# Second half unrolled, with x1, attention output and x2 split to 16-bit rows and transposed by DMA

## The chip, the core and the metric

The kernel runs on one core of a Trainium2 chip. The metric is the device time of one execution in microseconds (us). The core has five engines: TensorE (PE in the profile, its weight loads PEld), VectorE (DVE), ScalarE (ACT), GpSimd (POOL) and SyncE (SP), which here issues nearly all DMAs on one queue that 16 DMA engines serve. Engines wait for each other and for DMAs by semaphores, and each executes its instructions in order.

## The reference

One decoder layer, with the normalisation after each sublayer, over x (8 x 512 rows of 512) and a context (8 x 512 rows of 1024):

```
x1 = layernorm(x  + self_attention(x))          # over the axis of 8, 16 heads, relative positions
k, v = split(ctx @ W_src.T + b_src)             # 8 heads of 64, masked keys
q    = (x1 @ W_tgt.T + b_tgt) * mask
o    = softmax(q k.T / 8) v
x2 = layernorm(x1 + concat(x1, o) @ W_out.T + b_out)
out = layernorm(x2 + relu(x2 @ w1.T + b1) quantised @ w2.T + b2)
```

## The kernel before

Everything that TensorE multiplies in 16 bits is held as a pair of 16-bit tiles, a high part and a low part (value minus high part), and a product of two pairs is three matmuls (`terms`, line 44). A matmul contracts over partitions, so each activation that enters one must stand transposed, features on partitions.

The first half (`phase_a`, planned step by step by `FirstHalf`, line 301) computes x1 and the keys and values. It transposes its own activations by DMA: ScalarE writes the high part of a tile of 128 rows (`row_hi`, line 647), GpSimd the low part (`row_lo`, line 541), into one of a ring of three pairs `rows16`, and SP issues two DMA transposes (`turn`, line 455). DVE does the self-attention. x1 is stored as 32-bit rows in DRAM, keys (`kT_scratch`) and values (`v_scratch`) as 16-bit pairs.

The second half (`phase_b`, line 829) runs over the 8 batches b, each with 512 rows in four tiles tt of 128. Batch b of the attention is interleaved with the feed-forward of batch b-1 (`heads(b, ff)`, line 1146 on PE, 1287 on ACT, 1432 on DVE). At the boundary between two batches PE does, in this order:

- `feed_forward2` (four outputs of 16 matmuls with eight-bit operands), with the last head's `values` between the second and third;
- 16 transposes of the attention output o (`transposes`, line 1031, with the 32-bit identity, `b_st<-ident,k` and the like), one PSUM bank per tile; ACT and DVE make the pair `oT` from PSUM;
- `output_x1` (line 1134): 48 matmuls x1T by the first half of W_out, no end of the sum yet;
- the branch of the hardware loop (`Fori`), then 16 transposes of the next x1 (`x1_transposes`, line 1046), which SP loaded as 32-bit rows into `x1n` long before;
- `output_rest` (line 1184): 52 matmuls that add o's share and the bias; DVE adds the residual into `x2` (`residual`, line 1472), GpSimd makes the factors of the norm (`layer_norm_factors`, line 79), ACT applies them (`normalize`, line 1245);
- `queries` of the next batch (12 matmuls each), with 16 transposes of x2 ahead of the fourth, then the first scores, then `feed_forward1(ff, 0)`, the first reader of `x2T`.

SP's queue in the loop (lines 995 to 1003): the copies of the queries into `q1` and `q2` (18 DMAs in three groups, `queries`, line 953), the load of x1, mask and keys (`load_heads`, line 922, after the last `p_lo` of the batch) and values (five DMAs, after `av_filled`), the stores of four output tiles, and four loads of the residual rows (`load_residual`, line 947), each of which waits until the store from the same rows has landed. In the names of the profile `q` stands for what lives in `w.q` (x1n, x2) and also for q1/q2, `k` for what lives in `w.k` (o, pf) and k1/k2.

Of the kernel before, what the change touches and what calls it, by code (L numbers as in the profile page):

```python
# [64 lines left out]
def all_stored(sp, w):  # L65

    for i in range(2):
        sp.wait_ge(w.st_out[i], 16 * 2 * 8 * NBATCH // 2)
    for i in range(3):
        sp.wait_ge(w.x1_out[i], 16 * len(range(i, NB * T, 3)))  # L70

# [229 lines left out]
class FirstHalf:  # L301

    STEPS = 16 * NB + 4
# [33 lines left out]
    def uses(self, g):  # L337

        b, t = g // 16, g % 8
        out = [("o", n) for n in self.tiles(g - 1)]  # L340
        if b < NB - 1 and (1 <= g % 16 <= 8):
            out.append(("x", 8 * (b + 1) + g % 16 - 1))
        return out + [("c", n + 5) for n in self.quarters(g) if n + 5 < QUARTERS]
# [6 lines left out]
    def loads_after(self, g):  # L350

        return [use for use in self.uses(g + 1) if use[0] != "o"]
# [15 lines left out]
def phase_a(nc, ctx, d, w):  # L368
# [34 lines left out]
    turned = [sem(f"A_turned{i}") for i in range(RING)]  # L403
# [10 lines left out]
    x1_o = w.x1_d.rearrange("t (nb p) e -> nb t p e", p=P)  # L414

# [9 lines left out]
    def row_source(kind, i):  # L425

        return {"x": xn[i % 2], "c": cn[i % 2], "o": ctx1}[kind][:, :]
# [13 lines left out]
    with nc.Block() as block:  # L441
        @block.sync
        def _(sp):
# [11 lines left out]
            def turn(kind, i):  # L455
# [32 lines left out]
            def load_residual(n):  # L488
                if n >= 3:
                    sp.wait_ge(x1_out[n % 3], 16 * (n // 3))  # L490
                sp.dma_start(x1[n % 3][:, :], x_in[n // T, n % T]).then_inc(res_ld[n % 3], 16)
# [15 lines left out]
            for g in range(plan.STEPS):  # L507
# [17 lines left out]
                if g == 16 * (NB - 1) + 13 and w.b_ld is not None:  # L525
                    for n in range(0, NB * T, T):
                        sp.wait_ge(x1_out[n % 3], 16 * (n // 3 + 1))
                    sp.dma_start(w.x1n, w.x1_d.rearrange("b (tt p) e -> b p tt e", p=P)[0]).then_inc(w.x_ld, 16)
# [117 lines left out]
        def _(act):  # L646
            def row_hi(kind, i):
# [5 lines left out]
                elif kind == "c":  # L653
                    act.wait_ge(cn_ld[i % 2], 16 * (i // 2 + 1))
                else:
# [173 lines left out]
def phase_b(nc, ctx, d, w):  # L829
# [20 lines left out]
    x1n, x2 = w.x1n, w.q[:, 4:8, :]  # L850
    o, pf = w.k[:, 0:4, :], w.k[:, 4:8, :]
    x1T = pair("x1T", [P, KT, B])
# [36 lines left out]
    names = ("xt_filled", "xt_hi", "xt_lo", "q_filled", "q_masked", "q_hi", "q_lo", "m_made", "sx_filled", "sx_max",  # L889
             "negm", "mr_filled", "mr_copied", "st_filled", "st_exp", "p_hi", "p_lo", "av_filled", "o_rden",  # L890
             "o_norm", "ot_filled", "ot_hi", "ot_lo", "om_filled", "om_used", "x2t_filled", "x2t_hi", "x2t_lo",
# [7 lines left out]
    xr_ld = [sem(f"B_xr_ld{i}") for i in range(4)]  # L899
    out_st = [sem(f"B_out_st{i}") for i in range(4)]  # L900
    w1_ld, w2_ld = ([sem(f"B_{n}_ld{i}") for i in range(4)] for n in ("w1", "w2"))
    alone = {e: sem(f"B_alone_{e}") for e in ("sp", "dve", "pe", "act")}
# [15 lines left out]
    with nc.Block() as block:  # L918
        @block.sync
        def _(sp):  # L920
            def load_heads(b, first):

                if not first:
                    sp.wait_ge(s["p_lo"], 16 * b)
                    stand_alone(sp, alone["sp"])
# [8 lines left out]
                else:  # L934
                    sp.wait_ge(s["av_filled"], 8 * b)
                    stand_alone(sp, alone["sp"])
# [5 lines left out]
            def load_x1(b):  # L942
                sp.wait_ge(s["xt_filled"], 4 * b)
                stand_alone(sp, alone["sp"])
                sp.dma_start(x1n[:, :, :], x1_in[b]).then_inc(w.x_ld, 16)

            def load_residual(b, tt, first):
                if not first:
                    sp.wait_ge(out_st[tt], 16 * b)
                    stand_alone(sp, alone["sp"])  # L950
                sp.dma_start(x2[:, tt, :], x1_in[b][:, tt, :]).then_inc(xr_ld[tt], 16)

            def queries(b, g):
# [3 lines left out]
                stand_alone(sp, alone["sp"])  # L957
# [7 lines left out]
            def store(b, tt):  # L965
                sp.wait_ge(s["l3_done"], 4 * b + tt + 1)
                stand_alone(sp, alone["sp"])
# [20 lines left out]
            load_x1(1)  # L988
# [15 lines left out]
            last = NBATCH - 1  # L1004
            for g in range(len(GROUPS)):
                queries(last, g)
            for tt in range(4):
                store(last - 1, tt)
            for tt in range(4):
# [588 lines left out]
```

## Time and profile before

| | |
|---|---|
| median of 3 runs | 2004.89 us (2004.09 to 2007.42) |
| the profiled execution | 2004.7 us |
| its span in the trace | 2002.9 us |
| PE busy | 1861.0 us, 93% of the span |
| DVE busy | 1344.8 us, 67% |
| ACT busy | 784.5 us, 39% |
| POOL busy | 490.0 us, 24% |
| mean granted TensorE clock | 0.968 of 2.4 GHz |

The first half ends near 881 us of the span; the second half takes the rest. A matmul's record of 0.38 us overlaps its neighbours; how fast matmuls follow each other is read from the starts. A row of a timeline gives start, length, engine, line, operation, output<-inputs and count, and in brackets the idle time before it with what ended it. Rows of SPq are the issuing of DMAs on SP's sequencer, not the transfer; the time from issue to landing is listed apart.

### The profile page before, as it was taken

What the parts mean: (1) busy time and instruction counts of PE and PEld (TensorE: products, weight loads), DVE (VectorE), ACT (ScalarE), POOL (GpSimd) and SP (SyncE); (2) the same over time, 40 slices, a digit from 0 to 9 for tenths busy, and PEclk for the clock granted to TensorE, in tenths of its full rate; (3) what the DMA queues carried; (4) which work ended last, traced back from release to release, by engine and by line L of the source; (5) the groups of instructions that cost most, each with busy time, mean ns of one, the idle gap of its engine ahead of it and who ended that gap; (6) DMA issues with size and microseconds to landing.
All of it is one profiled execution on the core that took longest, in us unless ns stands there. A gap on an engine that the chain in (4) does not pass through costs nothing. (4 is left out here: it accounts for less than half of the span.)

```text
span 2002.9 us, 33372 instructions
## 1 busy us (share of the span) xinstructions
PE 1861.0 (93%) x12588; PEld 1022.7 (51%) x12588; DVE 1344.8 (67%) x1698; ACT 784.5 (39%) x1209; POOL 490.0 (24%) x546
## 2 busy tenths in 40 slices
PE   5998999899989897977899999999999999999998
PEld 5554565456545564544545545455455554554543
DVE  3499987898799879866665565564655555556531
ACT  3432222122222211136646265363562644635522
POOL 1334662475357423720000100001001000010010
PEclk7998999899989998989999999999999999999999
DMA  6543366335634445556420413304105142041010
GB/s 221 118 115 80 95 141 143 74 100 136 142 82 95 117 97 170 144 127 199 92 63 2 109 45 58 96 1 101 53 6 112 38 84 70 1 101 32 7 37 21
DMA packets 290831, 176.60 MB, mean 88 GB/s; under 512 B 194793, under 2 KB 248041, under 8 KB 290690
## 3 DMA queue, kind: packets, MB, share of 16 engines
q1 hardware_dynamic: 286320, 174.17, 34.6%
q8 instruction: 114, 1.87, 0.4%
q10 hardware_dynamic: 4370, 0.34, 0.2%
q14 instruction: 27, 0.22, 0.0%
HBM read 94.75 MB, written 33.55 MB: 64 GB/s over the span
## 5 line engine op out<-in xcount | busy, mean ns | idle before, releaser
L1351 DVE TENSOR_TENSOR p_lo<-k,p_hi 128x1024 f16<-128x1024 f32 x128 | 156.8, 1225 | 193.6 <-ACT p_hi L1239 193.6
L81 POOL TENSOR_TENSOR vsb<-mvb,consts 128x1 f32<-128x1 f32 x64 | 12.1, 190 | 1031.0 <-DVE mvb L1366 1031.0
L1040 PE MATMUL b_ff<-x2T_hi,w1T_hi 128*128 128x512 f16 x512 | 195.0, 381 | 2.3 <-DVE x2T_lo L1351 2.3
L1396 DVE CUSTOM_DVE_ANT_0 junk<-b_sx,mneg 128x512 f16<-128x512 f32 x256 | 175.8, 687 | 31.0 <-issue 22.4
L1040 PE MATMUL b_ff<-x2T_lo,w1T_hi 128*128 128x512 f16 x512 | 194.9, 381 | 0.0
L1040 PE MATMUL b_ff<-x2T_hi,w1T_lo 128*128 128x512 f16 x512 | 194.8, 381 | 0.0
L1271 ACT ACTIVATE k<-b_st,mbias 128x512 f32<-128x512 f32 x256 | 161.5, 684 | 15.0 <-PE b_st L1084 15.0
L619 PE MATMUL sm_b<-cT_hi,wsT_hi 128*128 128x256 f16 x512 | 143.4, 280 | 16.7 <-DMA cT_lo<-rows_lo 16.7
L741 DVE TENSOR_TENSOR prod<-q,k 128x4096 f32<-128x4096 f32 x32 | 141.9, 4433 | 22.0 <-ACT q L673 11.0
L1239 ACT ACTIVATE p_hi<-k 128x1024 f16<-128x1024 f32 x128 | 135.3, 1057 | 44.3 <-PE b_av L1099 41.9
L591 PE MATMUL pj_b<-winT_hi,xT_hi 128*128 128x512 f16 x384 | 146.6, 382 | 3.9 <-DMA xT_lo<-rows_lo 3.9
L1263 ACT ACTIVATE hq<-b_ff,b 128x512 fp8e4<-128x512 f32 x128 | 88.0, 687 | 156.0 <-PE b_ff L1040 149.1
L591 PE MATMUL pj_b<-winT_lo,xT_hi 128*128 128x512 f16 x384 | 146.6, 382 | 0.0
L591 PE MATMUL pj_b<-winT_hi,xT_lo 128*128 128x512 f16 x384 | 146.4, 381 | 0.0
L619 PE MATMUL sm_b<-cT_lo,wsT_hi 128*128 128x256 f16 x512 | 143.3, 280 | 0.0
L619 PE MATMUL sm_b<-cT_hi,wsT_lo 128*128 128x256 f16 x512 | 143.2, 280 | 0.0
L779 DVE TENSOR_TENSOR prod<-pr,v 128x4096 f32<-128x4096 f32 x32 | 142.1, 4442 | 0.5
L746 DVE TENSOR_REDUCE pr<-prod 128x128 f32<-128x4096 f32 x32 | 141.5, 4421 | 1.1
L1248 ACT ACTIVATE q<-q,rstdb 128x512 f32<-128x512 f32 x64 | 52.1, 814 | 161.7 <-POOL rstdb L87 161.7
L545 POOL TENSOR_TENSOR rows_lo<-ctx,rows_hi 128x512 f16<-128x512 f32 x32 | 86.6, 2705 | 115.4 <-ACT rows_hi L657 115.4
L1040 PE MATMUL b_ff<-w2T,hq 128*128 128x512 fp8e4 x512 | 112.9, 379 | 1.6 <-ACT hq L1263 1.0
L545 POOL TENSOR_TENSOR rows_lo<-cn,rows_hi 128x512 f16<-128x512 f32 x64 | 96.0, 1505 | 73.5 <-ACT rows_hi L657 73.2
(258 smaller groups left out, 4340.4 us busy)
## 6 DMA issues: line engine op xcount, KB each, us to landing
cn<-in_ctx_dram SPq DMA_DIRECT2D x64, 256.0 KB, 3.0
k<-kT_scratch SPq DMA_DIRECT2D x24, 512.0 KB, 7.8
xn<-in_x_dram SPq DMA_DIRECT2D x32, 256.0 KB, 2.9
x<-in_x_dram SPq DMA_DIRECT2D x32, 256.0 KB, 3.0
x_scratch<-x SPq DMA_DIRECT2D x32, 256.0 KB, 2.2
q<-x_scratch SPq DMA_DIRECT2D x8, 1024.0 KB, 5.6
q<-x_scratch SPq DMA_DIRECT2D x32, 256.0 KB, 3.9
out_dram<-q SPq DMA_DIRECT2D x32, 256.0 KB, 4.1
```

What stands on the lines that cost most here:

```text
L545: pool.tensor_tensor(lo[:, :], row_source(kind, i), hi[:, :], ALU.subtract).then_inc(s["row_lo"], 1)
L591: pe.matmul(out, a, c, start=(j == 0 and m == 0), stop=False)
L619: pe.matmul(dst, a, z, start=(j == 0 and m == 0), stop=False)
L741: dve.tensor_tensor(prod[:, :, :], q[:, t, :].unsqueeze(1).to_broadcast([P, T, E]), k[:, :, :], ALU.mult).then_inc(s["sc_prod"], 1)
L746: dve.tensor_reduce(pr[:, t].rearrange("p h s -> p s h"), prod[:, :, :].rearrange("p s (h d) -> p s h d", h=H1), AX.X, ALU.add).then_inc(s ...
L779: dve.tensor_tensor(by_head(prod), probs, by_head(v), ALU.mult).then_inc(s["av_prod"], 1)
L1040: mm = pe.matmul(out, a, c, start=(start and n == 0), stop=end)
L1239: act.activation(dst, src, ACT.Copy, scale=scale).then_inc(done, 1)
L1263: act.activation(hq[:, f, :], ff_b[f % 2][:, :], ACT.Relu, bias=b1[:, f:f + 1], scale=1.0 / WS, saturate=False).then_inc(s["relu"], 1)
L1271: act.activation(pf[:, st, :], st_b[st % 2][:, :], ACT.Exp, bias=mbias[:, st:st + 1], scale=D2 ** -0.5).then_inc(s["st_exp"], 1)
L1351: dve.tensor_tensor(dst, bank, hi, ALU.subtract).then_inc(out, 1)
L1396: dve.tensor_tensor_reduce(junk[:, :], sx_b[tt % 2][:, :], mneg[:, :], 1.0, NEG, ALU.add, ALU.max, mx[:, h % 2, tt:tt + 1]).then_inc(s["sx ...
```

## The change

- The loops of the second half over batches become plain Python loops, so every batch is written out; the `stand_alone` semaphore increments go.
- PE no longer transposes x1, o and x2. A ring of three pairs `rows16b` takes the high part (ACT, `row_hi`) and the low part (DVE, `row_lo`) of each tile of o and x2, from SBUF instead of PSUM, and SP issues two DMA transposes per tile (`turn`). A fourth tile waits until the first tile's transposes have landed.
- x1 is split to 16-bit rows already in the first half: a new kind of use "n" in its plan (ACT, GpSimd, then two DMA stores to `x1_rows_scratch`), one step longer. The second half reads x1 by eight DMA transposes per batch straight from DRAM (`turn_x1`), for batch 0 within the first half (`x1T_first`), alternating between two buffers.
- `output_x1` stands after `feed_forward2` in all batches. SP's queue is in another order.

```diff
+                if kind == "n":
+                    for z in range(2):
+                        sp.dma_start(x1r_o[z, i // T, i % T], rows16[u % RING][z][:, :]).then_inc(turned[u % RING], 16)
+                    return
...
-                    sp.dma_start(w.x1n, w.x1_d.rearrange("b (tt p) e -> b p tt e", p=P)[0]).then_inc(w.x_ld, 16)
+                    for tt in range(NB):
+                        for z in range(2):
+                            sp.dma_start_transpose(w.x1T_first[z][:, :, tt * P:(tt + 1) * P],
+                                                   w.x1r_d[z, 0, tt * P:(tt + 1) * P, :]).then_inc(w.x1_turned[0], 16)
...
+            def turn(kind, b, tt):
+                u = use_no(kind, b, tt)
+                dst = x2T if kind == "x2" else oT
+                sp.wait_ge(s["row_lo"], u + 1)
...
+                for z in range(2):
+                    sp.dma_start_transpose(col(dst[z], tt), rows16[u % RING][z][:, :]).then_inc(turned[u % RING], 16)
...
-            with sp.Fori(0, NBATCH - 2) as b:
-                for g in range(len(GROUPS)):
-                    queries(b + 1, g)
-                load_x1(b + 2)
-                load_heads(b + 2, False)
+            for b in range(NBATCH):
                 for tt in range(4):
-                    store(b, tt)
-                for tt in range(4):
-                    load_residual(b + 1, tt, False)
...
+                    turn("o", b, tt)
+                if b:
+                    for tt in range(4):
+                        store(b - 1, tt)
+                    for tt in range(4):
+                        load_residual(b, tt, False)
+                turn("x2", b, 0)
+                turn("x2", b, 1)
+                if b + 1 < NBATCH:
+                    queries(b + 1, 0)
+                turn("x2", b, 2)
+                turn("x2", b, 3)
+                if b + 1 < NBATCH:
+                    queries(b + 1, 1)
+                    queries(b + 1, 2)
+                if b + 2 < NBATCH:
+                    turn_x1(b + 2)
+                    load_heads(b + 2, False)
...
-                pe.wait_ge(s["o_norm"], 8 * b + 8)
-                for tt in range(4):
-                    transposes(tq_b[tt], o[:, tt, :], s["ot_filled"])
-                if ff is not None:
-                    output_x1(ff)
+                output_x1(b, ff)
...
+            def row_hi(kind, b, tt):
+                u = use_no(kind, b, tt)
+                if u >= RING:
+                    act.wait_ge(turned[u % RING], 32 * (u // RING))
...
                 normalized(b, H2 - 1)
+                for tt in range(3):
+                    row_lo("o", b, tt)
                 feed_forward_sum(ff, 2)
+                row_lo("o", b, 3)
                 feed_forward_sum(ff, 3)
...
-                for tt in range(4):
+                residual(b, 0)
+                for tt in range(1, 4):
                     residual(b, tt)
+                    row_lo("x2", b, tt - 1)
```

PE before, at the last boundary: L1033 are the transposes of o, then the matmuls of `output_x1` (wxT is W_out, x1T the transposed x1).

```order
L1099 MATMUL b_av<-v_hi,p_lo 128x65
L1040 MATMUL b_ff<-w2T,hq 128x512 x32
L1033 MATMUL b_st<-ident,k 128x128 x8
L1033 MATMUL b_mr<-ident,k 128x128 x4
L1033 MATMUL b_av<-ident,k 128x128 x4
L1040 MATMUL b_sx<-wxT_hi,x1T_hi 128x512
```

PE now, at the same place (L1075 and L1129 are lines of the changed kernel):

```order
L1129 MATMUL b_av<-v_hi,p_lo 128x65
L1075 MATMUL b_ff<-w2T,hq 128x512 x32
L1075 MATMUL b_sx<-wxT_hi,x1T_hi 128x512
L1075 MATMUL b_sx<-wxT_lo,x1T_hi 128x512
L1075 MATMUL b_sx<-wxT_hi,x1T_lo 128x512
```

The transposes are gone, and `output_x1` follows feed_forward2 directly.

SP before, in the loop from the last value load to the end of the body (ISA and REGISTER_ALU are address and count registers of the loop), and the queries that come next:

```order
L940 DMA v_lo<-v_scratch 128x4x512
L966 ISA
L968 ISA
L968 DMA out_dram<-q 128x512
...
L951 DMA q<-x_scratch 128x512
L995 REGISTER_ALU
L995 COMPARE_AND_BRANCH
L962 DMA q<-qn_hi 64x512 x2
```

SP now, for one of the batches in the middle:

```order
L960 DMA v_lo<-v_scratch 128x4x512
L971 DMA_TRANSPOSE oT_hi<-rows16b_hi 128x4x128
L971 DMA_TRANSPOSE oT_lo<-rows16b_lo 128x4x128
...
L999 DMA out_dram<-q 128x512 x4
L984 DMA q<-x_scratch 128x512 x4
L971 DMA_TRANSPOSE x2T_hi<-rows16b_hi 128x4x128
L971 DMA_TRANSPOSE x2T_lo<-rows16b_lo 128x4x128
...
L994 DMA q<-qn_hi 64x512 x2
L995 DMA q<-qn_lo 64x512
```

Between the value loads and the stores stand eight transposes of o; before the first group of queries stand four of x2, behind it four more.

DVE now, from the residual of the third tile to the first row part behind the queries (L1487 is the residual, L1363 the subtraction that makes a low part, L1393 the masking of a query tile):

```order
L1487 SCALAR_TENSOR_TENSOR q<-b_ff,q 128x512
L1375 BN_STATS statsb<-q 128x6
L1377 BN_AGGR mvb<-statsb 128x2
L1363 TENSOR_TENSOR rows16b_lo<-q,rows16b_hi 128x512
L1487 SCALAR_TENSOR_TENSOR q<-b_ff,q 128x512
...
L1363 TENSOR_TENSOR rows16b_lo<-q,rows16b_hi 128x512
L1393 SCALAR_TENSOR_TENSOR qf<-b_st,bt,mrow 128x512
L1363 TENSOR_TENSOR qn_lo<-qf,qn_hi 128x512
L1363 TENSOR_TENSOR rows16b_lo<-q,rows16b_hi 128x512
```

Before, the four residuals followed each other with nothing between them, and the low parts of x2 were taken from PSUM in one piece after the third query tile.

## Rows read from the trace of the kernel before

**Rows 1.** Stretches: us, busy time by engine, clock, DMA share, GB/s.
```profile
1147.00:1278.00 131.00, 127.65 (x960) 66.20 (x958) 74.47 (x154) 65.89 (x95) 8.94 (x32) 1.00 0.26 59
```

**Rows 2.** Timeline of PE at the boundary after batch 1: start us, length.
```profile
1108.68 7.07 PE L1040 MATMUL b_ff<-w2T,hq 128*128 128x512 fp8e4 x32
1115.59 1.04 PE L1033 MATMUL b_st<-ident,k 128*128 128x128 f32 x8
1117.33 0.38 PE L1040 MATMUL b_sx<-wxT_hi,x1T_hi 128*128 128x512 f16 x1
...
1128.45 1.09 PE L1033 MATMUL b_st<-ident,q 128*128 128x128 f32 x8 [0.59 <-issue]
...
1130.25 0.38 PE L1040 MATMUL b_sx<-wxT_hi,oT_hi 128*128 128x512 f16 x1
...
1149.24 1.04 PE L1033 MATMUL b_sx<-ident,q 128*128 128x128 f32 x8
...
1152.91 0.59 PE L1066 MATMUL b_sx<-k,q 128*128 128x512 f16 x2
...
1155.62 0.38 PE L1040 MATMUL b_ff<-x2T_hi,w1T_hi 128*128 128x512 f16 x1
```

**Rows 3.** Timeline of SP's issuing at the same boundary.
```profile
1108.99 6.78 SPq L938 DMA_DIRECT2D v_hi<-v_scratch  x4
1115.86 0.75 SPq L940 DMA_DIRECT2D v_lo<-v_scratch  x1
...
1122.97 2.17 SPq L951 DMA_DIRECT2D q<-x_scratch  x4
1146.58 1.18 SPq L962 DMA_DIRECT2D q<-qn_hi  x2
1147.80 0.59 SPq L963 DMA_DIRECT2D q<-qn_lo  x1
```

**Rows 4.** DMA transposes of the first half (L466): duration ns min/median/max, first and last.
```profile
L466 SPq DMA_TRANSPOSE cT_hi<-rows_hi x64: 1189/1212/1541, 73.5 to 829.4; - x64
L466 SPq DMA_TRANSPOSE cT_lo<-rows_lo x64: 1251/1264/2471, 74.8 to 830.6; - x64
...
DMA to landing us min/median/max: 2.4/2.5/5.3
```

**Rows 5.** Page, DMA issues: count, KB each, median us from issue to landing.
```profile
x_scratch<-x SPq DMA_DIRECT2D x32, 256.0 KB, 2.2
...
q<-x_scratch SPq DMA_DIRECT2D x32, 256.0 KB, 3.9
...
v_lo<-v_scratch SPq DMA_DIRECT2D x8, 512.0 KB, 5.8
...
q<-qn_hi SPq DMA_DIRECT2D x64, 64.0 KB, 2.0
```

**Rows 6.** Timeline of DVE and ACT: one residual, its norm, one split of queries.
```profile
1133.36 0.69 DVE L1476 SCALAR_TENSOR_TENSOR q<-b_sx,q 128x512 f32<-128x512 f32 x1 [1.10 <-PE b_sx L1042]
...
1134.92 0.18 DVE L1366 BATCH_NORM_AGGREGATE mvb<-statsb 128x2 f32<-128x6 f32 x1
...
1136.57 0.81 ACT L1248 ACTIVATE q<-q,rstdb 128x512 f32<-128x512 f32 x1 [5.37 <-POOL rstdb L87]
...
1145.13 0.63 ACT L1239 ACTIVATE qn_hi<-qf 128x512 f16<-128x512 f32 x1 [2.23 <-DVE qf L1383]
...
1145.79 0.69 DVE L1351 TENSOR_TENSOR qn_lo<-qf,qn_hi 128x512 f16<-128x512 f32 x1 [0.69 <-ACT qn_hi L1239]
```

**Rows 7.** Stretches of 2 us around a pause of PE; columns as in rows 1.
```profile
316.00:318.00 2.00, 0.00 (x0) 0.00 (x0) 2.00 (x1) 0.22 (x1) 0.46 (x2) 1.00 1.09 214
318.00:320.00 2.00, 0.71 (x7) 0.64 (x8) 0.91 (x1) 0.82 (x2) 2.00 (x3) 0.98 0.31 55
320.00:322.00 2.00, 2.00 (x11) 1.40 (x10) 0.75 (x1) 0.38 (x1) 1.07 (x1) 0.50 0.98 130
322.00:324.00 2.00, 2.00 (x14) 1.50 (x13) 0.00 (x0) 0.00 (x0) 0.00 (x0) 0.67 0.42 59
```

**Rows 8.** Waits of PE in the whole span: us in total, times, longest.
```profile
PE b_st L1040 <- DVE x1T_lo L1351: 3.9, 1, 3.9
```

**Rows 9.** SP in batch 0: its issue of w1's fifth block.
```profile
925.25 0.63 SPq L974 DMA_DIRECT2D x2T_hi<-in_w_dram  x1
```

**Rows 10.** GpSimd's split of o in the first half: duration ns min/median/max.
```profile
L545 POOL TENSOR_TENSOR rows_lo<-ctx,rows_hi x32: 1149/1156/5210, 183.3 to 866.7; 128x512 f16<-128x512 f32 x32
```

More of the change, by code:

```diff
@@ L342, in uses @@
             out.append(("x", 8 * (b + 1) + g % 16 - 1))
+        out += [("n", n) for n in self.tiles(g - 4)]
         return out + [("c", n + 5) for n in self.quarters(g) if n + 5 < QUARTERS]
@@ L402, in phase_a @@
     s = {n: sem("A_" + n) for n in names}
-    turned = [sem(f"A_turned{i}") for i in range(RING)]
+    turned = w.turned
     res_ld = [sem(f"A_res_ld{i}") for i in range(3)]
@@ L848, in phase_b @@
     ident16 = sb("ident16", [P, P], F16)
-    x1n, x2 = w.x1n, w.q[:, 4:8, :]
+    x2 = w.q[:, 4:8, :]
     o, pf = w.k[:, 0:4, :], w.k[:, 4:8, :]
-    x1T = pair("x1T", [P, KT, B])
+    x1T = [w.x1T_first, pair("x1T", [P, KT, B])]
+    rows16 = [pair(f"rows16b_{i}", [P, E]) for i in range(RING)]
     qf = [sb(f"qf{i}", [P, B], F32) for i in range(2)]
@@ L1021, in _ @@
             pool.memset(rows_b[:, :], 0.0).then_inc(s["made"], 1)
-            with pool.Fori(0, NBATCH) as b:
+            for b in range(NBATCH):
                 for l in ("l2", "l3"):
@@ L1221, in _ @@
             heads(0, None)
-            with pe.Fori(0, NBATCH - 1) as b:
-                x1_transposes(b + 1, False)
+            for b in range(NBATCH - 1):
                 output_rest(b)
@@ L1302, in heads @@
                     normalize("l3", ff, 1)
[L1303 to L1304 removed]
+                row_hi("o", b, 3)
                 if ff is not None:
@@ L1307, in heads @@
                     normalize("l3", ff, 3)
-            def x2_hi(b):
-                for tt in range(4):
-                    hi(col(x2T[0], tt), bank4(om_b[tt]), s["x2t_filled"], 4 * b + tt + 1, s["x2t_hi"])
             for z in range(2):
@@ L1466, in queries_and_first_maximum, with row_lo @@
                 queries_low(b, 3)
-            def x1_low(b):
-                for tt in range(4):
-                    low(col(x1T[1], tt), bank4(tq_b[tt]), col(x1T[0], tt), s["xt_hi"], 4 * b + tt + 1, s["xt_lo"])
+            def row_lo(kind, b, tt):
+                u = use_no(kind, b, tt)
+                src = x2 if kind == "x2" else o
+                low(rows16[u % RING][1][:, :], src[:, tt, :], rows16[u % RING][0][:, :], s["row_hi"], u + 1, s["row_lo"])
             def residual(b, tt):
@@ L1479, in residual @@
                 moments("l2", x2[:, tt, :], n, tt)
-            def x2_low(b):
-                for tt in range(4):
-                    low(col(x2T[1], tt), bank4(om_b[tt]), col(x2T[0], tt), s["x2t_hi"], 4 * b + tt + 1, s["x2t_lo"])
             dve.memset(q2[D2:P, :, :], 0.0).then_inc(s["rows_made"], 1)
@@ L1516, in _ @@
             last = NBATCH - 1
-            for tt in range(4):
+            residual(last, 0)
+            for tt in range(1, 4):
                 residual(last, tt)
-            x2_low(last)
+                row_lo("x2", last, tt - 1)
+            row_lo("x2", last, 3)
             for tt in range(4):
```

142 lines of the change are left out of this document (64 added, 78 removed).

## The prediction

> **What bounds the kernel now.** I read the busy times by stretch first. In the second half TensorE is busy 127.65 of 131 us in a batch, at full clock, while DVE has 74 and ACT 66 [rows 1]: the reader sees that an instruction taken off PE shortens the batch, until something else is late. Next comes PE's timeline at one boundary between batches, the only place that the change touches on PE [rows 2]. Read the starts, not the lengths. The two feed_forward2 outputs start at 1108.68 and end where the transposes of o start, at 1115.59: 32 matmuls in 6.91 us, 0.216 each. Then come 16 transposes until 1117.33 (1.74 us), output_x1 with 48 matmuls (10.4 us, to 1127.7), the loop's branch and the 16 transposes of x1 (2.55 us), output_rest from 1130.25, and the first matmul on x2T at 1155.62. The third view is SP's issuing at that boundary [rows 3], where I look for what stands ahead of the new transposes. The fourth is the one place where DMA transposes already run, the first half [rows 4], for the price of their issue and landing.
>
> **What is removed.** Per batch 1.74 us (o), 2.55 us (x1, with the branch and its 0.59 us of idle) and 1.74 us (x2; 16 transposes at the rate of the eight that start at 1149.24) [rows 2]: 6.0 us. Eight batches would give 48 us if all that replaces them were hidden. The stretch from 1115.59 to 1155.62 is 40.0 us long now and would be 34.0. Sixteen transposes in 1.74 us are 0.109 us each. The Trainium skill (TensorE: Matmul & The Clock Gate, Part 4: PE-mode transpose) gives about 275 ns for a transpose of 128 x 128 in a kernel, and by that figure 48 of them would be an estimated 13 us a batch and the ceiling over 100 us. By that rule a record has the right length here (eight of them make 1.04 us), but successive ones overlap, and the trace decides for 6.0 us.
>
> **What is added at a boundary.** I follow the chain for batch 1 in the clock of the trace. Everything new passes through SP in order.
>
> 1. SP issues the value loads until 1115.86 + 0.75 = 1116.6 [rows 3]. They wait for the last `values`, as do the rows of o, so nothing of o can be turned earlier. A pair of transposes takes SP 1.21 + 1.26 = 2.5 us [rows 4]. o0 is issued by 1119.1; v_lo, ahead of it in the same queue, lands 5.8 us after its issue [rows 5], at 1121.7. I let o0 land at 1122.2; by itself it would be 1120.4 (2.5 us after the second issue at 1117.9).
> 2. The ring has three slots, so the split of o3 waits for o0: ACT 0.63, DVE 0.69 [rows 6], 1123.6. Queued behind that on DVE is feed_forward_sum(3), for whose first operation (0.69) the last tile of output_x1 waits, since it writes the same bank. It could start at 1115.59 + 36 x 0.216 = 1123.4 and starts at 1124.4. PE loses 1.0 to 1.5 us, and output_rest starts at T = 1127.3 (11.7 us after 1115.59).
> 3. SP: o1, o2, o3 until 1126.6, then four stores. A load of the residual waits for the store of the same tile to land: 2.2 us at the best row for 256 KB, then 3.9 us for the load [rows 5]: 1126.6 + 2.2 + 3.9 = 1132.7, T + 5.2 or so. Before, these loads were issued at 1122.97 [rows 3], before output_rest had begun. Now residual(0), which PE allows at T + 2.8, is 2.4 us late.
> 4. A tile of x2 costs DVE 1.8 us (residual to moments, 1133.36 to 1135.1), 3.2 us from the residual's start to the norm on ACT, then 0.81, 0.63, 0.69 [rows 6]. DVE does residual(1), but before residual(2) it stands at the low part of tile 0: ready at 5.2 + 3.2 + 0.8 + 0.6 = 9.9, done at 10.6. Residual 2 from 10.6 to 12.4, low part of tile 1 to 13.1, residual 3 from 13.1, its norm 16.3 to 17.1. Low part 2 and the first masked queries end at 16.7; the high and low part of queries 0 end at 17.7 and 18.4; x2's fourth tile is split at 18.4 (ACT) and 19.1.
> 5. SP turned x2's tiles 0 and 1 meanwhile, then waits for those queries: six DMAs, 1.18 + 0.59 and so on, 3.7 us [rows 3], 18.4 to 22.1. Tile 2 to 24.6, tile 3 to 27.1, landed at 25.8 + 2.5 = T + 28.3.
> 6. PE meanwhile: output_rest 11.2, three queries 7.8, eight matmuls 1.7, so T + 20.7; the copies of the first queries land at 19.6 + 2.0 = 21.6 [rows 5], 0.9 us of wait. The scores and four matmuls take 2.7 us (1152.91 to 1155.62), and from T + 24.3 PE waits 4.0 us for x2T.
>
> So feed_forward1 starts 11.7 + 28.3 = 40.0 us after 1115.59: as before. The six microseconds go into waits. The sum hardly depends on where o0 lands: with T earlier by 1.3, the SP chain is late by as much against it. I bound the stretch by 38.3 (loads and stores at their fastest, 1.4 and 0.3 less) and 42.
>
> **The clock.** A pause of 3.6 us in the first half, from 315.7 to 319.3, is followed by the clock at 0.50 and 0.67 [rows 7], 1.2 instead of 2.4 GHz, for some 2.7 us, which is 1.35 us lost. A pause of 4.0 us does this too, I assume: 1.4 us a boundary, with 0 and 2.8 as bounds.
>
> **The other parts.**
> - Six boundaries (after batches 1 to 6): 6 x (0.0 + 1.4) = +8.4 us; bounds -10 and +24.
> - The boundary after batch 0 has output_x1 on the other side of the values now: o's transposes, 14 us behind `values`, are covered by 10.4 us of output_x1 only. There is no store there, so x2T comes at T + 26.9 instead of 25.4. I take +1.5 with the clock (-3 to +4).
> - After the last batch no value load and no query is in SP's way: 1.74 us saved on o, but x2T is complete 9.5 us after output_rest, where PE's transposes and the splits took 7.3: +0.4 (-1.7 to +3).
> - Batch 0: the 16 transposes of x1 and the wait for x1T_lo, 3.9 us [rows 8], go: about -5 with the clock. But SP issues eight transposes (10 us; one load of 0.4 us before) ahead of w1's fifth block, which went out at 925.25 [rows 9] and which PE was already waiting for. PE gets it some 9.6 - 5 us later than now, less what slack is left: +3 in all (-5 to +6).
> - The first half: at its end x1's last tile needs ACT 0.63, POOL 1.16 [rows 10] and two stores of 0.45, +2.7 us. Eight transposes hold SP for 10 us near the end, most of it in front of a row of o that had 7 us of slack, +1. Thirty-two more splits on POOL, 64 more issues on SP and a ring of three shared by one more user: +3 (0 to +11).
> - Semaphore increments gone on DVE and PE: -2 (0 to -3).
>
> Sum: 8.4 + 1.5 + 0.4 + 3 + 6.7 - 2 = +18 us on the profiled execution's 2004.7 (span 2002.9 and 1.8 around it; the median shown is 2004.89, the same): 2022.7, say 2022. The low ends together give 1985, the high ends 2055.
>
> **The rivals.**
> A. *The stretch shortens (the other side).* If stores and reloads land at their fastest, the clock holds over pauses of under 4 us and batch 0 keeps its 5 us, the low ends hold together: about 1987. For it: SP is idle from 1125.1 to 1146.6 now [rows 3], so nobody has tried how fast this path can be. Against: it needs several links at their minimum. The point from which it decides is residual(0) at T + 3.
> B. *The transposes cost SP no more than plain copies.* With 0.45 us an issue (four reloads took 2.17 us with their waits [rows 3]), o ends by 1125, residual(0) comes 1.6 us earlier and tiles 2 and 3 of x2 need 1.8 us instead of 5: x2T lands at T + 24.4, about when PE asks. Six boundaries give 3.9 us each, batch 0 keeps its 5, and the time is about 1975. 256 transposes at 1.19 us or more speak against it [rows 4]. The Trainium skill (Advanced Engine Details and Errata, X-Bar Transpose (TRN2)) says that transpose DMAs are as fast as regular ones; in landing the trace agrees (2.5 against 2.0 to 2.2 us), in issue it does not.
> C. *Everything is hidden*, PE is the bound: 2004.7 - 48 - 4 + 3 = about 1955. It needs x2T 5 us earlier than my chain gives.
> D. *Worse than forecast*: transposes from DRAM, which the trace of before does not show, or the ring in the first half hold SP and PE longer; 2045 or more.
>
> **How the numbers follow.** Forecast, 2008 to 2040: 0.56. A: 0.18. B: 0.06. C: 0.04. D: 0.09. That the parts cancel within 0.2% (4 us, about what a measurement of this kernel can tell from no change): 0.07. Faster is A, B and C, 0.28; same 0.07; slower 0.65. The range 1986 to 2042 leaves out B, C and most of D. The forecast's own range is 2008 to 2040.
>
> **What the profile would show.** Right: PE idles about 4 us ahead of each first matmul on x2T with the transpose DMA as releaser, and about 1 us inside output_x1 behind f16o; SP issues nearly without a gap from the value loads to the residual loads, and the query copies stand between two pairs of x2T; the clock dips once a batch; a batch takes about 132 us. Wrong: a batch of 127 us or less; transposes in the second half at 0.5 us an issue; or a first half longer by over 15 us.

## The result, and the profile after

| | before | changed |
|---|---|---|
| median | 2004.49 us (2003.41 to 2007.42, 4 runs) | 2045.26 us (2042.59 to 2045.66, 4 runs) |
| span of the profiled execution | 2002.9 us | 2043.3 us |
| PE busy | 1861.0 us | 1833.9 us |
| POOL busy | 490.0 us | 536.0 us |
| mean granted clock | 0.968 | 0.955 |

The ratio is 1.0198, 95% interval 1.0181 to 1.0216: 41 us slower, where +18 was forecast and 2042 was the upper end of the range. The direction was right, and the forecast size was less than half of what came.

The stretches of the changed kernel, columns as in [rows 1]. The first is one whole batch, the second the boundary just before it (from the end of feed_forward2 to feed_forward1), the third its feed_forward1 and heads:

```profile
1180.26:1315.29 135.03, 125.81 (x917) 62.35 (x917) 72.36 (x151) 65.25 (x92) 9.65 (x32) 0.98 0.33 73
1138.46:1180.26 41.80, 33.48 (x154) 14.66 (x152) 20.35 (x41) 10.33 (x15) 7.22 (x23) 0.99 0.55 131
1180.26:1258.13 77.87, 77.04 (x652) 39.97 (x653) 41.70 (x92) 49.68 (x70) 0.00 (x0) 0.96 0.14 30
```

PE has 125.8 busy in 135.0 us, where it had 127.65 in 131 [rows 1]. The third row, 77.87 us with PE busy nearly all of it and a clock of 0.96, was 76.1 us long before. PE's timeline at the boundary after batch 1, which answers to [rows 2]:

```profile
1138.46 0.38 PE L1075 MATMUL b_sx<-wxT_hi,x1T_hi 128*128 128x512 f16 x1
...
1147.95 0.39 PE L1075 MATMUL b_ff<-wxT_hi,x1T_hi 128*128 128x512 f16 x1 [1.56 <-DVE f16o L1435]
...
1153.14 0.38 PE L1077 MATMUL b_sx<-rows_b,ones 128*128 128x512 f16 x1
...
1173.38 0.59 PE L1096 MATMUL b_sx<-k,q 128*128 128x512 f16 x2 [1.95 <-DMA q<-qn_lo]
...
1180.26 0.59 PE L1075 MATMUL b_ff<-x2T_hi,w1T_hi 128*128 128x512 f16 x1 [4.47 <-DMA x2T_lo<-rows16b_lo]
```

SP's issuing there, which answers to [rows 3]:

```profile
1131.75 8.31 SPq L958 DMA_DIRECT2D v_hi<-v_scratch  x4
1140.10 0.79 SPq L960 DMA_DIRECT2D v_lo<-v_scratch  x1
1141.00 1.23 SPq L971 DMA_TRANSPOSE oT_hi<-rows16b_hi  x1
...
1150.18 1.27 SPq L971 DMA_TRANSPOSE oT_lo<-rows16b_lo  x1
1151.49 2.04 SPq L999 DMA_DIRECT2D out_dram<-q  x4
1153.77 2.69 SPq L984 DMA_DIRECT2D q<-x_scratch  x4
1162.34 1.63 SPq L971 DMA_TRANSPOSE x2T_hi<-rows16b_hi  x1
...
1170.03 1.16 SPq L994 DMA_DIRECT2D q<-qn_hi  x2
...
1173.85 1.22 SPq L971 DMA_TRANSPOSE x2T_hi<-rows16b_hi  x1
...
1177.72 1.27 SPq L971 DMA_TRANSPOSE x2T_lo<-rows16b_lo  x1
```

Read the two together. SP issues without a gap from 1131.75 to 1156.46, the picture that the forecast drew: values, then o, then stores, then reloads. PE stands idle for 1.6 us inside output_x1, for 1.95 us before the first scores and for 4.5 us before its first matmul on x2T. The waits of PE in the whole span (us in total, times, longest):

```profile
PE om_b L614 <- DMA c1T_lo<-rows_lo: 47.5, 8, 10.4
PE b_ff L1075 <- DMA x2T_lo<-rows16b_lo: 40.1, 8, 9.2
...
PE b_ff L1075 <- DVE f16o L1435: 10.7, 6, 2.5
PE b_sx L1096 <- DMA q<-qn_lo: 10.3, 7, 1.9
PE b_ff L1068 <- DMA x2T_hi<-in_w_dram: 9.2, 1, 9.2
```

The second row is the wait for x2T at the seven boundaries (3.8 to 4.7 us each) and behind the last batch (9.2). The rows of f16o and of the query copies belong to the boundaries too. The last row is the fifth block of w1 in batch 0. The transposes of o and x2 have the issue time and the landing time of those in the first half [rows 4]:

```profile
L971 SPq DMA_TRANSPOSE oT_hi<-rows16b_hi x32: 1207/1220/1298, 1011.7 to 1951.4; - x32
...
L971 SPq DMA_TRANSPOSE x2T_lo<-rows16b_lo x32: 1190/1267/1274, 1029.0 to 1975.7; - x32
...
DMA to landing us min/median/max: 2.3/2.4/4.6
```

Where the 40.4 us between the two spans are, by the starts on PE:

| part | forecast | measured |
|---|---|---|
| first half (881.10 to 889.59) | +6.7 | +8.5 |
| batch 0 and the boundary behind it (first matmul on x2T: 1024.15 to 1046.30, less the 8.5) | +4.5 | +13.7 |
| six middle boundaries (131.78 to 134.79 a batch) | +8.4 | +18.1 |
| last boundary and the end | +0.4 | +0.2 |
| increments gone | -2 | inside the other rows |

Batch 0 has three waits of PE that it did not have before, or not at this length: the 9.2 us for w1's fifth block (1.7 before), 3.9 us for the last `p_lo`, and 5.2 us for the first oT, behind the keys and values on SP:

```profile
997.94 0.20 PE L1126 MATMUL b_av<-v_hi,p_hi 128*128 128x65 f16 x1 [3.92 <-DVE p_lo L1363]
...
1016.73 0.61 PE L1075 MATMUL b_sx<-wxT_hi,oT_hi 128*128 128x512 f16 x1 [5.22 <-DMA oT_lo<-rows16b_lo]
```

```profile
1000.80 9.91 SPq L958 DMA_DIRECT2D v_hi<-v_scratch  x4
```

### The profile page after: what moved, and what is told of

It reads as the page before. It is cut to its first block, busy times and chain, and to the rows that moved or that the text cites. A ratio compares the mean times of both kernels' runs of the same rounds, so it can differ in the third digit from the quotient of the medians.

```text
span 2043.3 us, 30887 instructions
## 1 busy us (share of the span) xinstructions
PE 1833.9 (90%) x12204; PEld 987.1 (48%) x12204; DVE 1329.4 (65%) x1666; ACT 791.5 (39%) x1209; POOL 536.0 (26%) x578
## 4 chain that ended last, share of the span: by engine, by line
PE 31%; SPq 8%; DVE 5%; DMA 5%; ACT 4%; issue 2%; POOL 1%; ACTq 0%; DVEq 0%; POOLq 0%
PE b_ff L1075 19%; SPq L971 3%; SPq L958 3%; PE b_st L1113 2%; PE b_st L1114 2%; PE b_sx L1096 2%; PE b_av L1126 2%; PE b_av L1129 1%; PE b_av L1127 1%; DVE p_lo L1363 1%; SPq L994 1%; DMA x2T_lo<-rows16b_lo 1%; DMA q<-x_scratch 1%; DMA oT_lo<-rows16b_lo 1%; PE b_sx L1075 1%
## 5 line engine op out<-in xcount | busy, mean ns | idle before, releaser
L1363 DVE TENSOR_TENSOR p_lo<-k,p_hi 128x1024 f16<-128x1024 f32 x128 | 156.6, 1223 | 192.6 <-ACT p_hi L1253 192.6
L1075 PE MATMUL b_ff<-x2T_hi,w1T_hi 128*128 128x512 f16 x512 | 200.4, 391 | 40.1 <-DMA x2T_lo<-rows16b_lo 40.1
L1075 PE MATMUL b_ff<-x2T_hi,w1T_lo 128*128 128x512 f16 x512 | 200.2, 391 | 0.0
L1075 PE MATMUL b_ff<-x2T_lo,w1T_hi 128*128 128x512 f16 x512 | 200.1, 391 | 0.0
L756 DVE TENSOR_TENSOR prod<-q,k 128x4096 f32<-128x4096 f32 x32 | 141.9, 4433 | 20.6 <-ACT q L688 12.1
L558 POOL TENSOR_TENSOR rows_lo<-cn,rows_hi 128x512 f16<-128x512 f32 x64 | 104.3, 1633 | 65.1 <-ACT rows_hi L672 64.5
L1075 PE MATMUL b_ff<-w2T,hq 128*128 128x512 fp8e4 x512 | 113.0, 379 | 0.8 <-ACT hq L1276 0.8
L1126 PEld LDWEIGHTS b_av<-v_hi,p_hi 128*128 128x128 f16 x1024 | 93.4, 98 | 32.8 <-DVE p_lo L1363 28.2
L1126 PE MATMUL b_av<-v_hi,p_hi 128*128 128x65 f16 x1024 | 101.1, 196 | 7.6 <-DVE p_lo L1363 7.4
```

Source lines behind the costliest of these rows:

```text
L558: pool.tensor_tensor(lo[:, :], row_source(kind, i), hi[:, :], ALU.subtract).then_inc(s["row_lo"], 1)
L756: dve.tensor_tensor(prod[:, :, :], q[:, t, :].unsqueeze(1).to_broadcast([P, T, E]), k[:, :, :], ALU.mult).then_inc(s["sc_prod"], 1)
L1075: mm = pe.matmul(out, a, c, start=(start and n == 0), stop=end)
L1126: pe.matmul(dst, hi[:, st, rows], v_hi[:, st, h, :], start=(st == 0), stop=False)
L1363: dve.tensor_tensor(dst, bank, hi, ALU.subtract).then_inc(out, 1)
```

## The experiments

Theory S: what is lost is lost in SP's in-order queue and in what PE waits for behind it. The rivals were that the unrolled program is slower by itself (U), that the split, norm and low-part chain of DVE and ACT sets the boundary (L), and that the clock has no part in it (K). Two more belong to one run each: that the first half loses its time by the eight transposes from DRAM and not by the rows (P), and that w1 is late for another reason than the transposes ahead of it (W). Each ratio is to the kernel before, on the same chip, with its 95% interval. Differences in us are between medians. The medians of the kernel before lay between 2003.08 and 2004.49 beside these runs, so differences under some 3 us say nothing.

**The unrolling alone.**

```
-            with pe.Fori(0, NBATCH - 1) as b:
+            for b in range(NBATCH - 1):
...
-                    stand_alone(pe, alone["pe"])
```

> The kernel before with its second-half loops written out and the lone semaphore increments gone, nothing else. Theory S (the change loses its time in SP's in-order queue and in what PE waits for behind it): the unrolling itself gives a little, seven loop branches of 0.6 us of idle on PE and some increments on DVE, so 2004.5 - 2 to - 5, 1999 to 2003 us. Rival U (the written-out program is slower by itself, for instance because instructions arrive late): 2008 us or more, and PE waits on its own sequencer in the second half.

1990.09 us, ratio 0.9922 (0.9906 to 0.9939). U is refuted, and the gain that S gave it was too small by 9 us (1999 at the low end). The edit takes out the loops and the `stand_alone` increments together, so their shares stay unknown. One batch of it:

```profile
1152.92:1282.80 129.88, 128.15 (x965) 66.81 (x964) 75.21 (x156) 66.78 (x96) 9.00 (x32) 1.00 0.24 60
```

A batch was 131.78 us on average. At the branch, output_x1 to the transposes of x1 now takes 10.36 us (1115.46 to 1125.82) where it took 11.12 to 12.02; feed_forward1 with the heads takes 75.39 in place of 76.14. So against a kernel with the same loops written out, the rest of the change costs 55 us, not 41.

**The first half alone**, and the same without the stores.

```
+        out += [("n", n) for n in self.tiles(g - 4)]
...
+                    act.wait_ge(s["ln_done"], i + 1)
```

> The kernel before with only the first half's part: x1 is also split on ACT and GpSimd and stored as 16-bit rows, which nobody reads. Theory S with the sizes of the forecast: the ring of three and GpSimd cost 3 us and the tail 2.7, so 2009 to 2012 us. Rival P (the first half's loss comes from the eight transposes of batch 0's x1 from DRAM in SP's queue): 2006 us or less.

2008.78 us, 1.0026 (1.0016 to 1.0037): 5.2 us by the ratio, where the forecast had 5.7 for this part. P wanted 2006 or less and is refuted.

```
-                        sp.dma_start(x1r_o[z, i // T, i % T], rows16[u % RING][z][:, :]).then_inc(turned[u % RING], 16)
+                    sp.sem_inc(turned[u % RING], 32)
```

> The kernel before with x1 split to 16-bit rows in the first half (ACT, GpSimd, ring, as in the run that cost 5.0 us) but the rows not stored: SP only marks them as gone. If the 5 us are SP's 64 issues and their transfers, 2004 us (before itself: 2003.5). If they are GpSimd's 32 splits and the order of the ring, 2007 to 2009 us.

2006.77 us, 1.0017 (1.0005 to 1.0030), between the two cases expected. The two intervals overlap, so the times do not tell the parts apart. The profiles, one execution each, have PE's first transpose of the second half at these starts (before; split only; split and stored; changed kernel):

```profile
881.10 1.94 PE L1033 MATMUL b_sx<-ident,q 128*128 128x128 f32 x8 [4.75 <-PEq L441]
```

```profile
881.88 1.94 PE L1043 MATMUL b_sx<-ident,q 128*128 128x128 f32 x8 [6.28 <-PEq L445]
```

```profile
885.63 1.94 PE L1044 MATMUL b_sx<-ident,q 128*128 128x128 f32 x8 [7.19 <-PEq L445]
```

```profile
889.59 1.94 PE L1068 MATMUL b_sx<-ident,q 128*128 128x128 f32 x8 [7.20 <-PEq L445]
```

That is 0.8 us for the splits, 3.7 for the stores and 4.0 for what is left in the changed kernel, batch 0's eight transposes from DRAM in place of one load. It speaks for SP rather than GpSimd, but it is one execution of each, and no run has the eight transposes alone.

**Batch 1's x1 behind the weights.**

```
-            turn_x1(1)
             sp.wait_ge(s["wq_filled"], 4)
...
             for n in range(4, FT):
                 load_weights(n)
+            turn_x1(1)
```

> The changed kernel with the eight transposes of batch 1's x1 behind the last weight load of w1 and w2 instead of ahead of the fifth. Theory S: PE's wait of 9.2 us at the fifth block of w1 goes, down to the 1.7 us of before, and the half speed behind it: 2045.3 - 7.5 - 1 = 2037 us. Rival W (weights are late for another reason, the link or the slots they are loaded into): the wait stays over 5 us and the time within 3 us of 2045.

2034.41 us, 1.0141 (1.0124 to 1.0158), 10.9 less than the changed kernel, where 8.5 were expected. The wait for w1's block is gone, and W is refuted. The wait for oT in batch 0 stays (5.9 us). The fifth block's issue in the changed kernel, behind eight transposes and four reloads, and here:

```profile
937.90 1.26 SPq L978 DMA_TRANSPOSE x1T_lo<-x_rows_scratch  x1
939.21 2.00 SPq L984 DMA_DIRECT2D q<-x_scratch  x4
941.59 0.34 SPq L1005 DMA_DIRECT2D x2T_hi<-in_w_dram  x1
```

```profile
927.27 1.85 SPq L984 DMA_DIRECT2D q<-x_scratch  x4
929.17 0.43 SPq L1005 DMA_DIRECT2D x2T_hi<-in_w_dram  x1
```

**The value loads behind the residual loads**, and the key loads alone moved there.

```
+                if b + 1 < NBATCH:
+                    load_values(b + 1)
                 turn("x2", b, 0)
                 turn("x2", b, 1)
```

> The changed kernel with the five value loads of the next batch issued after the residual loads, no longer ahead of the transposes of o. Theory S: o is turned 9 us earlier, the wait inside output_x1 (1.2 to 2.5 us) goes, the residual loads are there when output_rest has its first tile, and x2T comes 2.5 us earlier after that: 1.5 + 2.5 us a boundary and 1 us of clock, seven boundaries, 2045.3 - 35 = 2010 us, from 2005 to 2022. Rival L (the latency of residual, norm, split and transposes of x2 on DVE and ACT sets the end, not SP's queue ahead of them): only the wait in output_x1 goes, PE still waits 4.5 us for x2T, 2045.3 - 10 = 2035 us.

2005.95 us, 1.0012 (1.0002 to 1.0022): 39.3 less. S had 35, and L is refuted for the part ahead of x2. The gain is not where S had it, though: the clock gives almost nothing back (the heads still take 77.07 us), and 9.3 us of it lie in batch 0, where PE no longer waits for oT (first matmul on x2T at 1036.99 after 1046.30). The keys alone:

```
+                if b + 1 < NBATCH:
+                    load_keys(b + 1)
                 turn("x2", b, 0)
                 turn("x2", b, 1)
```

> The changed kernel with only the three key loads (512 KB each) moved behind the residual loads; the value loads stay ahead of o's transposes. In the changed kernel SP issues the four value loads in 8.3 us behind the keys, in the kernel with later values in 3.7 us. If this is the queue standing full of the keys, the values now take 3.7 us to issue, o is turned 4.6 us earlier, the wait inside output_x1 goes, and about half of the 39 us of the later values are gained: 2045.3 - 18 = 2027 us, 2018 to 2034. If the values' issue takes its 8 us by itself when they stand there, 2040 us or more.

2006.88 us, 1.0013 (1.0002 to 1.0023): 38.4 less, twice what I expected, and as much as by moving the values. SP with the keys moved:

```profile
1123.44 4.09 SPq L962 DMA_DIRECT2D v_hi<-v_scratch  x4
1127.58 0.78 SPq L964 DMA_DIRECT2D v_lo<-v_scratch  x1
1128.46 1.24 SPq L975 DMA_TRANSPOSE oT_hi<-rows16b_hi  x1
```

The four value loads take 4.09 us in place of 8.31 (2.8 to 4.2 us at all seven boundaries, 7.7 to 9.9 in the changed kernel). So half of the values' issue time came from the 1.5 MB of keys in front of them. In the changed kernel the third value load holds SP until 1138.0, and the last key load lands at 1138.6. That would fit a queue that takes no more while it is full, but no run shows its depth. The first row of o goes out at 1128.46, 1.7 us ahead of the end of feed_forward2 (1130.15). In the changed kernel it went out 2.5 us behind it. The boundary is 37.6 us (1130.15 to 1167.73) after 41.8. The chain takes the 4.2 us whole. Moving the values too gives it nearly nothing more (37.3): residual(0) then starts 3.0 us after output_rest, as early as PE allows, and with the keys moved it is 3.8. In both kernels PE still waits for x2T, 3.8 to 4.0 us with later values and 3.8 to 5.0 with later keys, and the heads still take 77 us.

**Is it the issue of a transpose?** Two kernels: plain copies of the same bytes in place of the transposes of o and x2, and one transpose for high and low part together. The first leaves out the turning itself, so its output is not the layer's.

```
-                    sp.dma_start_transpose(col(dst[z], tt), rows16[u % RING][z][:, :]).then_inc(turned[u % RING], 16)
+                    sp.dma_start(col(dst[z], tt), bank4(rows16[u % RING][z])).then_inc(turned[u % RING], 16)
```

> The changed kernel with the DMA transposes of o and x2 replaced by plain copies of the same bytes between the same buffers, so that nothing is turned there (x1's transposes from DRAM stay). Theory S (the issue time of a transpose on SP, 1.25 us against some 0.5, is what the boundary pays): the wait inside output_x1 goes (1.6), x2T comes 3 to 4 us earlier and the half clock behind the pause goes (1.7), seven boundaries of 6 to 7 us: 2045.3 - 45 = 2000 us, 1990 to 2008. Rival L (latency of the split and norm chain on DVE and ACT): PE still waits over 3 us for x2T, 2035 us or more.

2024.02 us, 1.0089 (1.0068 to 1.0111): 21 less. An issue takes 0.62 us. The time lies between what S (1990 to 2008) and L (2035 or more) had, and neither is borne out. The values are still in front, the fourth tile still waits for a place in the ring of three (f16o, 2.1 us on average), and pauses of 1.9 to 3.4 us remain before x2T.

```
+                sp.dma_start_transpose(col(both, tt), rows_both[u % RING][:, :]).then_inc(turned[u % RING], 16)
```

> The changed kernel with one DMA transpose of 128x1024 for the high and the low part together in place of two of 128x512 for o and x2. If SP's 1.25 us are a price for each issue, half of them go and the time is near that of the kernel with plain copies, 2000 to 2010 us. If they are a price for the elements, an issue takes 2.5 us, the high part can no longer go before the low one is ready, and the time stays within 6 us of 2045.

2014.59 us, 1.0058 (1.0041 to 1.0074): 31 less. Twice the elements cost SP one issue:

```profile
L972 SPq DMA_TRANSPOSE oT<-rows16b x32: 1232/1262/3331, 1008.9 to 1917.0; - x32
L972 SPq DMA_TRANSPOSE x2T<-rows16b x32: 1232/1250/1692, 1024.8 to 1943.9; - x32
```

PE waits 1.6 to 2.7 us for x2T here. Behind four of the seven pauses (1.6 to 2.3 us) the heads take 75.35 us, behind the other three (2.3 to 2.7) about 77.0. That is 6.8 of the 12.6 us by which its profiled execution beats that of the plain copies, where all seven are 76.6 or more.

**The clock alone.** 18 extra matmuls where PE waits for x2T.

```
+                        for j in range(18):
+                            pe.matmul(ff_b[0][:, :], col(wxT[0], 0)[:, j % KT], wxT[0][:, j % KT, :],
+                                      start=j == 0, stop=j == 17)
```

> The changed kernel with 18 extra matmuls (3.9 us at 0.216 each, their result is overwritten) on PE at the seven places where it waits 3.8 to 4.7 us for x2T. Theory S with the clock: feed_forward1 and the heads after it take 77.0 to 77.9 us in the changed kernel and 75.4 in the unrolled one of before; if the half clock after the pause makes this difference, the extra work gives back 1.6 to 2.5 us a boundary although nothing else is faster: 2045.3 - 13 = 2032 us, 2028 to 2037. Rival K (the longer stretch has another cause, DMA traffic or the order of ACT and DVE): 2045 us or more.

2031.78 us, 1.0142 (1.0114 to 1.0170): 13.5 less, by doing more work, whose result is overwritten. K is refuted. Stretches of 2 us on PE (busy, count, clock, DMA share, GB/s) around the wait, the changed kernel and this one:

```profile
1176.00:1178.00 2.00, 0.00 (x0) 1.00 0.59 107
1178.00:1180.00 2.00, 0.00 (x0) 0.78 0.42 94
1180.00:1182.00 2.00, 1.74 (x5) 0.50 0.36 92
1182.00:1184.00 2.00, 2.00 (x6) 0.50 0.42 106
```

```profile
1174.00:1176.00 2.00, 2.00 (x11) 1.00 0.75 125
1176.00:1178.00 2.00, 1.47 (x7) 1.00 0.34 76
1178.00:1180.00 2.00, 1.95 (x10) 1.00 0.39 98
```

In the changed kernel the clock falls from 1.00 (2.4 GHz) within the wait and is at 0.50 (1.2 GHz) from 1180 to 1184. With the extra work it stays at 1.00, and feed_forward1 with the heads takes 75.35 to 75.37 us at all seven boundaries, after 76.87 to 77.87. Over the seven that is 14 us, the whole gain.

**The first query group on ACT's queue.**

```
-                if b + 1 < NBATCH:
-                    queries(b + 1, 0)
...
+                act.wait_ge(s["q_lo"], 4 * (b + 1) + 1)
+                for a in range(2):
...
+                        act.dma_start(dst, qn[0][rows, 0:1, :]).then_inc(qs_ld[0][a], 16)
```

On the changed kernel:

> The changed kernel with only the first query group's six copies on ACT's queue; the value loads stay ahead of o's transposes. Theory S: in the changed kernel x2's third tile is ready before the copies and waits behind them, so x2T is 4 us early here too, and the loss inside output_x1 stays: 2045.3 - 7 x (3.8 + 1.7) = 2007 us, 2003 to 2016. Rival L (what is behind the value loads is late by itself, so that the copies only fill a gap): less than 12 us gained, 2033 us or more.

2017.35 us, 1.0075 (1.0046 to 1.0104): 28 of the 38 expected. The wait for x2T is gone at the seven boundaries and every head stretch is 75.38, but other waits around the first scores have taken a part of it: 17.1 us for the query copies (10.3 in the changed kernel) and 13.8 us for `mxb`, the maxima that DVE makes (4.0). On the kernel with later values:

> The changed kernel with the value loads behind the residual loads (2006.0 us) and the six copies of the first query group issued on ACT's queue instead of between two pairs of x2's transposes on SP. Theory S: x2's last pair is issued 4 us earlier, PE's wait of 3.8 us for x2T and the half clock behind it (1.7) go at seven boundaries: 2006 - 38 = 1968 us, 1965 to 1978. Rival L: x2T is late because the norm's chain is, and gains 1 us at most; or ACT's issuing delays the next query splits and the wait only moves: 1995 us or more.

1979.26 us, 0.9880 (0.9864 to 0.9897): 26.7 less than 2005.95, where 38 were expected. A batch is 125.2 to 125.6 us. L is refuted for the second part of the boundary too; the waits for `mxb` (12.9 us after 3.5) are most of what is missing.

**x1 alone.** The unrolled kernel of before, x1 through DRAM rows, o and x2 turned by PE.

```
-                x1_transposes(b + 1, False)
...
-                    pe.wait_ge(s["xt_lo"], 4 * b + 4)
+                    pe.wait_ge(x1_turned[b % 2], 128 * (b // 2 + 1))
```

> The unrolled kernel of before (1990.1 us) with only x1 taken over: 16-bit rows stored by the first half, turned from DRAM, batch 1's eight transposes behind the last weight load; o and x2 are still turned by PE. Theory S: x1's transposes stand in SP's queue where SP has nothing urgent, so all of PE's 1.74 us a batch are gained: 1990.1 + 5 (rows in the first half) + 2 (eight transposes near its end) - 8 x 1.74 - 4 (PE's wait for x1T in batch 0) = 1979 us, 1975 to 1986. Rival D (transposes from DRAM slow what runs beside them): 1990 us or more.

1981.38 us, 0.9883 (0.9867 to 0.9900), within the 1975 to 1986 expected. A batch:

```profile
1153.97:1282.11 128.14, 126.42 (x950) 65.05 (x949) 72.72 (x152) 64.72 (x92) 9.01 (x32) 1.00 0.27 61
```

It is 1.74 us shorter than in the unrolled kernel, the whole price of PE's sixteen transposes.

**All together.** The moves of w1_first, v_later and q_act, and for batch 0:

```
+                if ff is None:
+                    output_x1(b, ff)
                 values(b, H2 - 1)
```

> All the moves together: batch 1's x1 behind the weights (-10.9 alone), value loads behind the residual loads (-39.3), first query group on ACT's queue (-26.7 on top of that), and for batch 0 output_x1 ahead of the last values as in the kernel before (PE waits 3.9 us there for p_lo). If the causes are separate places of one queue, the gains add: 1979.3 - 10.9 - 4 = 1964 us, 1960 to 1969. If they share a cause, 1972 us or more.

1974.24 us, 0.9853 (0.9825 to 0.9880): 5 less than q_act, not 15 (the two profiled executions are 0.6 apart). The first matmul on x2T comes 4.1 us earlier in batch 0 (1029.71 after 1033.79; oT is waited for 6.6 us now that the values stand last), and then heads at 77.08 us instead of 75.38 at two boundaries more give most of it back. One such stretch, and the next:

```profile
1280.66:1357.74 77.08, 75.98 (x654) 39.55 (x653) 44.75 (x100) 50.36 (x71) 0.00 (x0) 0.98 0.13 29
1407.98:1483.36 75.38, 74.44 (x654) 39.02 (x653) 44.74 (x100) 50.37 (x71) 0.00 (x0) 1.00 0.13 29
```

What makes the clock fall at some of these boundaries and not at others stays open: PE's waits for `mxb` just before are 1.35 and 0.46 us ahead of the first row and 1.34 and 0.45 ahead of the second.

With the single transpose of the kernel one in addition:

> The same as comb with one transpose of 128x1024 for the high and low part of each tile of o and x2. Alone this gave 31 us on the changed kernel. Theory S: PE no longer waits for SP at the six boundaries in the middle, so half the issue time is worth nothing there; only the boundary after the last batch (9.3 us of wait) and batch 0 get some: 0 to 3 us less than comb. Rival: SP's queue still holds something PE waits for at each boundary, then 8 us or more less than comb.

1968.21 us, 0.9824 (0.9798 to 0.9851): 6 less than comb, between the two cases (3.6 between the profiled executions; the intervals of the two kernels overlap). All seven head stretches are 75.34 to 75.36 us, and the last boundary waits 8.4 in place of 9.4. A batch:

```profile
1156.45:1282.01 125.56, 123.03 (x917) 61.47 (x917) 72.54 (x152) 65.14 (x92) 9.96 (x32) 1.00 0.36 78
```

This version beats both kernels: 1.8% under the kernel before, 77 us under the changed one.

## Why the prediction was right in sign and wrong in size

The forecast missed by 22 us: 9.7 in the six middle boundaries (step 1 of the chain), 9.2 in batch 0, 1.8 in the first half, and the 2 us of the increments, whose gain lies within the other rows. Unrolling was worth 14 us, and without it the miss would have been larger by about 12. The signs by which it was to be known as right (idle before x2T, about 1 us behind f16o, SP without a gap) all came, with 4.5 us for 4 and 1.6 for 1. They did not tell the size, and a batch took 134.8 us for the 132 named with them.

1. **What is removed: held.** The 48 transposes a batch are gone (384 matmuls fewer in all), and x1's 1.74 us show alone (x1_only). The Trainium skill (TensorE: Matmul & The Clock Gate, Part 4: PE-mode transpose) gives about 275 ns for a transpose of 128 x 128 in one kernel; an estimate from that figure makes the batch 4.4 us shorter without 16 of them. The trace has 1.74.
2. **The chain at a boundary: right in order, and step 1 was mis-sized.** The forecast had 40.0 us from the end of feed_forward2 to feed_forward1, as before. At this boundary it is 41.8; over the six it is 42.1 on average, where the kernel before has 40.4. Step 1 had SP through with the values 1.0 us after feed_forward2's end, taken over from [rows 3]; they end 2.4 us after it, since the four loads took 8.31 us and not 6.78. They take 8.07 us in the unrolled kernel of before too, where nobody waits for it. Everything behind moved by that: T at 12.1 for 11.7, residual(0) at T + 6.4 for 5.2, the query copies at T + 19.5 for 18.4, x2T at T + 29.7 for 28.3. The sentence that the sum hardly depends on where o0 lands misled: the landing is not the link, but the issue of o0 is, and k_later shows that with o0 issued 4.2 us earlier against feed_forward2 the stretch ends 4.2 us earlier. Six times 1.7 (42.1 less 40.4) is 10.3 us. The clock's part came 0.1 under its 1.4 a boundary, and together that is the 9.7 us missed there.
3. **The clock: the mechanism was right, its size a little small.** Against heads of 75.38 us the pause costs 1.5 to 2.5 us a boundary, where 1.4 was taken from [rows 7]. The rows themselves give more: 2 us at 0.50 and 2 us at 0.67 are 3.3 us at half speed, 1.7 us lost. The upper bound of the six boundaries was also added up too low: 6 x (2 + 2.8) is 29, not 24. Against the kernel before only 1.2 remain, because the unrolling gave 0.75 back in the same stretch.
4. **Unrolling: mis-sized.** I put -2 on the increments and left the branch in the 2.55 us of x1's transposes. It is worth 13.7 us, increments and loops together. This hid part of a larger loss: a batch of the changed kernel is 4.9 us longer than in the unrolled kernel, not 3.0.
5. **Batch 0: the other step that failed.** The forecast had +3 for batch 0 and +1.5 for its boundary; it is 13.7. The text named one cause, eight transposes ahead of w1's fifth block [rows 9], but set 5 us of gain and some slack against it. PE waits 9.2 us there after 1.7, and w1_first gets 10.9 back. The block goes out 16.3 us later (941.59 after 925.25), of which 8.5 are the first half's. Of the wait for x1T that I credited, 3.9 us [rows 8], most stays: PE waits 2.9 us for wxT_lo at the same place. The wait of 3.9 us for `p_lo`, which output_x1 covered before, had no term. The wait for oT was mis-sized: the sum had 14 us of transposes against 10.4 us of output_x1, and the keys and values in front of them left 5.2 us. Behind that wait PE ran at half speed (clock 0.50 from 1016 to 1022), so x2T came 29.6 us after the start of output_rest and not 26.9; with later values, where PE does not wait for oT, it comes 27.0 us after it.
6. **The first half: +6.7 forecast, 8.5 measured.** The rows cost 4.5 us at the start of the second half where 5.7 were said. The eight transposes near the end cost 4.0 and not 1, as far as one execution of each kernel tells.
7. **The rivals.** A needed residual(0) at T + 3; it came at T + 6.4. With later values it does come at T + 3.0, and the boundary of 37.3 is then below the 38.3 that the forecast had as its bound, but the clock still falls. B fell with the issue time: 1.22 and 1.27 us, as in the first half. The Trainium skill (Advanced Engine Details and Errata, X-Bar Transpose (TRN2)) calls transposes as fast as regular DMAs. The trace agrees in landing (2.3 to 2.4 us for those of x2, 2.3 for the plain copies in their place). In issue it has 1.25 against 0.62, and the kernel with one transpose a tile shows that this is a price for each DMA, not for its elements. C is what comb_one nearly reaches (1968 against 1955), but only with the queue in another order, and with 14 us from unrolling that the forecast had at 2. D gave the number (2045), but by SP's queue in batch 0 and at the boundaries more than by what it named, the transposes from DRAM and the ring of the first half.

## What to carry to other kernels

When work moves from a busy engine to DMAs, write out the issuing queue in order and price each issue. Here 1.25 us for a transpose, 0.6 for a copy and 8 us for value loads behind 1.5 MB of keys decided, while the time from a transpose's issue to its landing (2.4 us) stayed what it was. Loads that nobody needs for a while belong behind the issue that the next engine waits for; moving three key loads gave back 38 of the 41 us. And let one part of a change run alone: here two good parts (unrolling, -14; x1, -9) stood beside one whose queue order lost it all.

## What the runs showed of the hardware beyond what was expected

- A DMA transpose of 128x1024 holds SP for 1.25 us (kernel one), as one of 128x512 does (1.22 to 1.27).
- Issuing slows behind large loads: the same four value loads took 8.31 us behind three loads of 512 KB, 4.09 without them.
- The hardware loops and the `stand_alone` increments together cost about 1.9 us a batch on PE, 0.75 of it spread over the stretch of feed_forward1 and the heads (76.14 to 75.39).
- Doing 3.9 us of useless matmuls in a wait made the kernel 13.5 us faster over seven waits, since the granted clock stayed at 1.00.
